# A new order of 1027 steps in a two-layer macaron block on one core

## The reference, cut to what matters

```python
x = x + 0.5 * int8_ffn(layernorm(x))        # rows quantised to int8, 128x128 weight, bias
x = x + attention0(layernorm(x))            # 16 heads of width 8, rotary, causal
x = x + 0.5 * int8_ffn(layernorm(x))
x = x + 0.5 * gated_ffn(layernorm(x))       # silu(gate) * up, hidden width 384
x = x + attention1(layernorm(x))            # 16 heads of width 64, causal
x = x + 0.5 * gated_ffn(layernorm(x))
```

## Time and profile before

| | us |
|---|---|
| median of 3 runs | 766.88 |
| lowest and highest | 765.96, 769.78 |
| the profiled execution, own time | 767.49 |
| its span in the trace | 765.7 |
| PE busy, share of the span | 696.4, 91% |
| DVE busy | 577.0, 75% |
| POOL busy | 499.2, 65% |
| ACT busy | 445.5, 58% |

### The profile page before, as it was taken

One profiled execution on the slowest core, in us unless ns is written; L12 is line 12 of the kernel. 1 busy time (PEld: TensorE's weight loads), 2 busy tenths in 40 slices (PEclk: granted clock), 3 DMA queues, 4 the chain that ended last, 5 costly groups with the idle time before them and its releaser, 6 DMA issues. The chain is left out here.

```text
span 765.7 us, 21921 instructions
## 1 busy us (share of the span) xinstructions
PE 696.4 (91%) x9509; PEld 413.8 (54%) x9511; DVE 577.0 (75%) x808; ACT 445.5 (58%) x536; POOL 499.2 (65%) x387
## 2 busy tenths in 40 slices
PE   2756888888889899999999999999999999999997
PEld 1523445444444454565655556556667555566774
DVE  7698897898998886778778777665676766774286
ACT  2333665988777769545655756555624565655511
POOL 6862245506854410389899999968981979999910
PEclk9856998999999999999999999999999999999999
DMA  8000000000000000001001011011101101101010
GB/s 275 8 1 2 3 2 3 2 3 3 2 3 3 2 3 3 3 3 30 3 30 30 3 29 32 4 29 30 31 3 30 30 3 30 30 6 45 12 29 29
DMA packets 13015, 15.68 MB, mean 20 GB/s; under 512 B 3000, under 2 KB 10488, under 8 KB 12920
## 3 DMA queue, kind: packets, MB, share of 16 engines
q1 hardware_dynamic: 12344, 13.96, 6.4%
q10 hardware_dynamic: 576, 0.33, 0.1%
HBM read 12.74 MB, written 1.16 MB: 18 GB/s over the span
## 5 line engine op out<-in xcount | busy, mean ns | idle before, releaser
L742 ACT ACTIVATE Pr<-ps 128x1024 f32<-128x1024 f32 (+1 forms) x258 | 237.8, 965 | 96.0 <-PE ps L1345 50.0
L1171 DVE TENSOR_REDUCE mxb<-ps 128x8 f32<-128x1024 f32 (+1 forms) x147 | 172.1, 1194 | 72.5 <-PE ps L1345 44.4
L725 POOL TENSOR_TENSOR V0s<-V0s,Pr 128x1024 f32<-128x1024 f32 x66 | 161.9, 2453 | 63.0 <-PE ps L1294 46.9
L1140 DVE TENSOR_REDUCE big<-ps 128x8 f32<-128x1024 f32 (+1 forms) x166 | 171.5, 1077 | 24.0 <-PE ps L1324 15.3
L1345 PE MATMUL ps<-big 64*128 64x128 f16 (+2 forms) x2560 | 169.0, 259 | 2.8 <-DVE mxb L1171 1.4
L1324 PE MATMUL ps<-big 32*128 32x128 f16 (+2 forms) x1280 | 102.0, 276 | 35.7 <-DVE big L1140 21.5
L1345 PEld LDWEIGHTS ps<-big 64*128 64x128 f16 x2560 | 92.1, 94 | 65.3 <-issue 22.1
L1324 PEld LDWEIGHTS ps<-big 32*128 32x128 f16 x1280 | 42.7, 95 | 108.6 <-ACT Pr L742 36.1
L1294 PE MATMUL ps<-Pr,V1s 128*64 128x256 f32 (+2 forms) x704 | 92.9, 404 | 0.4 <-ACT Pr L742 0.4
L725 POOL TENSOR_TENSOR acts<-acts,Pr 128x1024 f32<-128x1024 f32 x30 | 73.8, 2461 | 10.7 <-PE ps L1294 5.6
L1264 PE MATMUL ps<-Pr,V0s 128*18 128x128 f32 (+2 forms) x1280 | 80.3, 378 | 0.3 <-ACT Pr L749 0.3
(11 more groups left out here) (261 smaller groups left out, 1034.8 us busy)
## 6 DMA issues: line engine op xcount, KB each, us to landing
rec_b<-scratch_dram SPq DMA_DIRECT2D x28, 256.0 KB, 3.9
X<-in_x_dram SPq DMA_DIRECT2D x2, 256.0 KB, 3.5
big<-in_pick_rows_dram SPq DMA_DIRECT2D x2, 256.0 KB, 3.7
X<-in_x_dram SPq DMA_DIRECT2D x1, 512.0 KB, 6.3
rec_b<-in_w_q_dram SPq DMA_DIRECT2D x1, 512.0 KB, 6.1
XT<-in_w_k_dram SPq DMA_DIRECT2D x1, 512.0 KB, 6.9
XT<-in_w_v_dram SPq DMA_DIRECT2D x1, 512.0 KB, 8.0
wo_s<-in_w_o_dram SPq DMA_DIRECT2D x1, 512.0 KB, 9.2
```

The lines of the kernel that those rows point to most:

```text
L725: g.tensor_tensor(dst, dst, src, ALU.add).then_inc(summed, 1)
L742: ins = a.activation(dst[:, part], src, func, scale=scale)
L1140: ins = v.tensor_reduce(maxima_of(mall[:, r, 2 * u:2 * u + 2][:, part], i), block_view(src, i), AX.X, ALU.max, negate=True)
L1171: ins = v.tensor_reduce(maxima_of(mxb[:, r][:, part], arg), block_view(src, arg), AX.X, ALU.max, negate=True)
```

## The change

The string `ORDER` is replaced. Both strings have 1027 letters, with the same count of each. The first three steps, steps 402 to 463 except for one swap of `pq` and `pk` (the end of stage one), and the last 17 steps are at the same places; nearly all others are moved by some places against the other streams. Through `deal_banks()` the banks of the moved steps change too: 53 steps instead of 46 get two banks that aren't neighbours (`exp` 4 instead of 1, `max` 4 instead of 3, `gexp` 16 instead of 17, and one each of `pq`, `pk`, `gkq` and `imm` instead of none).

The diff:

```diff
--- before.py
+++ after.py
@@ -214,17 +214,17 @@
 
 
 ORDER = (
-    "hhammmmmmhmmmmmmmmmamammmmmtememeeemhemmwmmwehemwemwmememwememewmeeheemwtmhmwhememwmheewemamewehmege"
-    "mwemwmemwmhmmmhmeemewehemtemmwemwhmhhhmhmememwhemewmegeemwhmhemewmhemwmeaeewmtememwmeememwemwmemwmee"
-    "emahewemwememewemewemmemwhemmtwwhemgemememwhemmwemgewmmhhamhheewehmewehmmewehemwmmhewememtwemememwme"
-    "amhemhhwemwemeeehmwememwmemwemwememheheewwmehtehhhhhhhwhhhwehmemgemhemwemeehwemwememewmemwemwememewm"
-    "mhhewmmQKQtVVMegeeMweMeweMeweMeweMeweMeweMeweeMgeewTKKQwwMMgEEEMWWMEEMWMMhMEEMEEMQKhTWhhWWWMEhMhhWWM"
-    "EMWSMEEEMWMEEMEEMMWWMMTWQhMWWMEMWWMEEMVhVhhVKWWWTSMEhEEMWMEEEEMWMMMWWWWMEEEEMQKhMWWWMEMWWSTMEMWMEEEh"
-    "hMWWWEhMKQhWWMEEMhEhVSTMEMWEEEEMWWWMMMWhWWMEhKQhhWWMhhEEMEhTSMEEhMWhWEMMWWMEEMWWWMEEEMVhWWEQKVSTEEMM"
-    "WWMEEEMWWMMMWWWMEEMEEESTQKWWWMMWWMEEEEMWMMMWWWMEEMEQVKVWWSTEMEEMWWMEEMEMWWWWWMEEEEEMWWMEEMQOKOSTMMWW"
-    "WEMMWWMMVQVKOOMMWWEMESThhEEMEEMEEEEMWWMMVhKQhWWWMMMWWWWEMEEEMSTMEEWWMEEEMKhWWWWMMMhWWWMEEMEhQVhhhWWT"
-    "SEMEEMWWMEEEMVhQhKhWhWWWWhMEEMWMMMWWEEMSTMEMWWMEEEEMWWWWMEEEMWWWWMEEMESTEEWWWWWEEVEEEEWWWWWXOXEEXFXh"
-    "FFEOFWWWWLXLLFXOFOLFFLFLLLL"
+    "hhammmmmmmmmmmmmmammmmmmmtamemmemmeeheemwhmemwmeewmmewmhewmemhemewemetwmemwmeheewemehhhwemewmamegeem"
+    "wmemweemhmwmmhmemmewemewmewmhhmhthmemhhmehmemwemmwmegeemhmhhwmewmemeameweemeweemwmteewmememwmemwemem"
+    "heewemwememaemwmeewemmhwmewmetmhwmegememehmwmemwemgehmmhmamhheeweemhwheemwmemwehemweemmwemwemtmhwmea"
+    "mmhehemwemweemewehhhemwemewemewemewemmmheetwmehhhhhhhwhhhehhmwmegmehememwmehhewemewemewemewmemwememw"
+    "mmhewmmKQQtVVMegeeMweMeweMeweMeweMeweMeweMeweeMgeewTKKQwwMMgEEEMWMEMWMMVhMEEMEEMETWMMQhKWWWWhMEhMhWW"
+    "hSMhEEMWMEEMEEMEMWTMEMWhVhKQWWWWWhMEMWMhEEMWhWMEEMTSMEEEMWWWMEEMWMMQhVKhhWWWMEEMEEEMMWWMMhEWEMSThhVh"
+    "WWWMEEMWhWWMEEEMhhVKhQWWMETSEhhMMWWMEEEEMWWWWWMMQVKhEhEEhMWWWWMEEMMWTSMEEMWWMEEMWWMEEhMMWWWQKVSTMEEE"
+    "EEMWWWEMMWWMEMWMEEQKWWMEEMEEMSTWWWWMEEEMWWWMEEEEMWWMEMWMMVQKVSTEMEEMWWWMEMWWWMEEEEEEEWWWMMKQOOMMOSTM"
+    "WMEMWWMMVKQOMEMhhWWWMEEMEEEMMWWMMMWWWTSMEEEEMVhQKhWhhhWWWMEEMEEEMMWWWWMSTMEMWMEEEMhKVQhWWWWMEEMEEMEM"
+    "WWMSTEMMWWWWMEEhEMWWWMEEEMKhQWWWSTMEEEhMWWWWMEEEhVVWWMhEEMWWMhEMWMEEMESTEEWWWWWWEEEEWWWWXEEOXEEXEXFW"
+    "hFFOFLWWWWXLLFXOFOLFFLFLLLL"
 )
 LEFT = {letter: iter(steps) for letter, steps in streams().items()}
 PLAN = [next(LEFT[letter]) for letter in ORDER]
```

## The result

The new kernel takes 774.28 us (median of 4 runs, 773.37 to 778.13) against 766.94 for the kernel before (765.96 to 769.78): ratio 1.0099, 95% interval 1.0056 to 1.0142. It is slower by about 1%, or 7.3 us by the medians. The prediction had said 765.2 us, with a range that ended at 771.5. The profiled execution took 773.37 us, its span is 771.6 us.

The account below looks back on a forecast made before the run. PE, 91% busy, was taken as full in stage two, DVE as fullest in stage one. 767.49 - 2.95 (first shift) - 2.9 (cluster) + 4.3 (end) = 765.9, stated as 765.2 us for runs; range 758.5 to 771.5.

Parts of the forecast that it names:

- For all the other gaps I take no change: Stage one, DVE's gaps outside the first shift and the 117 to 136 us cluster: no change taken.
- First shift: Stage one, near 62 us: `gkq 2` and one `gmax` fill PE's 2.89 us idle, closing DVE gaps; 2.95 us won.
- Cluster at 117 to 136 us: Stage one, 5.8 us of DVE gaps before 12 `gmax` instructions: half of it, 2.9 us, won.
- a bigger gain than I took: Stage one, hole at 62 us: by the clock-gate rule, filling it should win more than the 2.95 us taken.
- DVE's collision with POOL: Stage one cluster, line 1147 beside POOL's rotary multiplications: 1.25 us collision comes again, shrinking the half taken to 1.7 us.
- Stage two: 312 to 728 us: PE is full, so its time is kept; bounds 3 us won, 4 us lost.
- PE above 98% busy: Sign for stage two, together with the same length within 3 us.
- POOL's queue: Late stage two: later releases and three moved `split` steps put POOL's last addition at 732.4 instead of 731.11.
- The end: Line 1205 waits for POOL ahead of 18.3 us of DVE work; last layernorm 4.3 us later, bounds 0 and 5.5.
- rival C: Slower: line 1205's wait lowers PE's clock, end costs 8.9 us, stage one wins only 2.95; 772.8 us, chance 0.24.
- B: Rival: the end does not shift, as DVE finds POOL's last addition done; 761.0 us, chance 0.13.
- A: Rival: more out of stage one, a third of DVE's remaining 27.4 us of gaps closed; 759.1 us, chance 0.20.

Follow-up runs that it names:

- the one letter alone: Kernel before with `exp` (15,8), and so line 1205, moved ahead of `lsum` (14,1), `down` (5,0) and `lturn`, `lwo` of (15,0): 771.43 us, ratio 1.0058.
- the letter put back: New kernel with `exp` (15,8), and so line 1205, back behind `down` (5,0) and `lturn`, `lwo` of (15,0): 773.78 us, ratio 1.0083 against the kernel before.
- undoing all: New kernel with its last 45 steps in the order of the kernel before: 769.58 us, ratio 1.0032 against the kernel before.
- 252+: Kernel before with only its first 252 steps in the new order: 764.27 us, ratio 0.9950.

## Why the prediction was wrong

The pieces that cover the whole list, each measured alone, against the terms of my sum (us, from the ratios times 767):

```
steps           mine                 measured (95% interval)
0 to 251        -2.95 - 2.9          -3.8 (-5.1 to -2.6)
252 to 401       0                   +3.2 (+1.8 to +4.7)
402 to 849       0 (-3 to +4)        +2.4 (+1.5 to +3.1)
850 to 981   \                       +1.2 (+0.4 to +2.1)
982 to 1026  /  +4.3                 +3.2 (+2.1 to +4.3)
sum             -1.6                 +6.2, and all in one +7.6 (+4.3 to +10.9)
```

**The step that failed** is "For all the other gaps I take no change: the same steps at other distances, which can go either way". In steps 252 to 401 the new order costs 3.2 us (1.8 to 4.7), where I had nothing. My bound for the whole of stage one beyond the first shift was 4 us lost, but I put these gaps at zero with no better reason than that they can go either way, and I did not read the new list for how many PE and ACT steps stand between two `gmax`, where the rows on line 1140 above show DVE's waits. Next to it stand stage two, kept at zero, with 2.4 us, and steps 0 to 251, whose gain I took 2 us too high.

**First shift,** 2.95 us: won 1.1. The mechanism was right on DVE (no gap of 0.9 us behind `gexp` 0(0,0) at once; PE's 2.89 us are gone), and the term mis-sized: it left out that with `gkq 2` gone from its old place the clock stays at half between 56 and 62 us, and one DVE gap of 1.42 us opened at 71.59 us in the new kernel. I had written that PE's clock made the filled hole "a bigger gain than I took". It was a smaller one.

**Cluster at 117 to 136 us,** 2.9 us: won 0.7 behind the new first 60 steps (1.8 - 1.1), lost 1.2 alone. In the new kernel's trace the wait is elsewhere: PE stands 1.73 us before `gexp` 1(8,0) at 120.61 and runs `v` at half clock, 3.39 us from 122.71. DVE's collision with POOL came again too, on the neighbouring line. Timelines of DVE and POOL in the new kernel:

```profile
117.14 1.97 DVE L1146 TENSOR_SCALAR big<-big 128x32 f16<-128x32 f32 x1
119.14 0.19 DVE L1147 SCALAR_TENSOR_TENSOR big<-big 128x32 f16<-128x32 f32 x1
```

```profile
116.69 2.37 POOL L693 TENSOR_TENSOR V1s<-V1s,turns 128x1024 f32<-128x1024 f32 x1
```

Line 1146 takes 0.18 us for groups 0 and 1 of the same kernel (at 60.05 and 86.42, where POOL does nothing), and here 1.97 us, until POOL's instruction ends at 119.06. The Trainium skill, SBUF — State Buffer (Who interferes with whom), says that a `tensor_scalar` that uses both of DVE's ports and a GpSimd instruction block each other fully; the trace agrees, within 0.1 us.

**Stage two,** "I take its time as kept": it lost 2.4 us, inside my bound of 4. I had asked for PE above 98% busy as a sign; it is 97.9% (407.1 of 416). PE was 98.9% busy before; a full engine says that an order can't win, and it says nothing against a loss.

**POOL's queue.** Pair 12 was to start at 649.9 and starts at 650.73; pair 13 at 672.0, and it starts at 672.41; the last addition was to end at 732.4 and ends at 732.88. The count of releases was right.

**The end,** 4.3 us: steps 850 to 1026 cost 1.2 + 3.2 = 4.4 us in the old list, and the one letter alone 4.4. The size is right. The mechanism at line 1205 is right in the old list, but not the whole: I had priced it at 18.3 us of DVE's work and left PE's clock to rival C, and of the one letter's 4.4 us about 1.5 are half clock. The 1.3 us of POOL's later end came too, but by PE's wait before `weigh` (15,7). In the new kernel there is PE's wait before `wo` 1 (0,6,0) as well, and with the letter put back nearly nothing came back. That wait was in the list to be read, one `weigh` less ahead of a step that depends on POOL, and I looked at DVE's queue only. So that the sum for the end came out to 0.1 us is luck in part.

**The rivals.** B did not come: line 1205 waits 4.87 us. Nor did A, which needs 12 us out of stage one; the first 252 steps alone win 3.8. C named the right side: the end costs more than stage one wins. Its 772.8 us is 1.5 us from the measured time, but by errors that cancel: its end of 8.9 us was too high, its stage one of 2.95 us won too kind, and it had nothing for stage two. The half clock after a wait at the end, which C asked for, shows in two of the experiments, and at `fxt` 0 in the new kernel. The page TensorE: Matmul & The Clock Gate (HAM oscillation — how this bites in real kernels) of the Trainium skill says that waits between bursts bring the clock down; the trace agrees, with 3.64 and 4.00 us for a step of 2.17. It doesn't hold each time: in the new kernel itself `wo` ran at full clock after the same 3.01 us, and the clock fell only at `fxt` 0, behind a wait of 2.22 us.

**Open.** The five pieces sum to 6.2 us and the whole is 7.6, within the intervals. What the 1.9 us between steps 252 and 298 come from I haven't shown by a run, nor the part of each stage-two wait. Nor is it shown by a run what keeps the time up when the one letter is put back in the new kernel; one trace points to the half clock.

## What to carry to other kernels

When a list orders several queues, check for each consumer how much of the producer's time stands between two of its inputs, and compare it with the consumer's own time: 1.8 us between reductions of 1.22 us is a wait of 0.6 in each round, although all engines have as much to do as before. Price the end of a kernel from the last external release onward on every engine, and not only on the one that looks tight: a late product of one engine can reach the end by several ways, and undoing one move gave back 0.5 us where undoing all gave 4.7. An order that is tuned whole can be worse while its first part is better: splice old and new where both have done the same set of steps, and keep the winning part (here 0.5% faster than the kernel before by the ratio, 0.3 to 0.7).

## What the runs showed of the hardware

The same instructions do not always get the same clock. The experiments with the new first 60 steps and with the new steps 402 to 849 have the same list from 60 to 401, and stand at the same time to 0.01 us from 152 to 165 us. Timelines of PE, first the one, then the other:

```profile
164.04 1.07 PE L1480 MATMUL ps<-idh_s,big 128*128 128x128 f16 x16
...
165.61 1.91 PE L1264 MATMUL ps<-Pr,V0s 128*18 128x128 f32 x32
...
168.00 1.43 PE L1264 MATMUL ps<-Pr,V0s 128*18 128x512 f32 x8
```

```profile
164.03 1.07 PE L1480 MATMUL ps<-idh_s,big 128*128 128x128 f16 x16
...
165.52 1.07 PE L1264 MATMUL ps<-Pr,V0s 128*18 128x128 f32 x32
...
166.86 1.05 PE L1264 MATMUL ps<-Pr,V0s 128*18 128x512 f32 x8
```

The first fell to 1.2 GHz at about 165.3 us, with waits of only 0.53 and 0.65 us on PE in the 5 us before, and stood 1.3 us behind from 170 to 184 us; the other went on at 2.4 GHz. Such falls of the clock are most of the jumps of the table above: over 160 to 168 us the granted clock is 0.79 in the "252+" kernel and 1.00 in the new one, with the same list up to there. Over 93 runs of the kernel before, taken beside the experiments (765.07 to 769.71 us), time and the run's mean granted clock (0.961 to 0.975) go together with a correlation of -0.78, 0.3 us for each 0.001. So part of what an order is worth in stage one is how often it meets such a fall. By an estimate from one or two falls of 1.2 to 1.3 us, a single trace can't tell less than about 2 us apart.
